# Attention's row of maxima: from sixteen products and four copies to one product, one copy and one transfer; three pairs loaded ahead

## The reference

```python
x = x + 0.5 * ffn(layernorm(x), w_router, w_gate, w_up, w_down)   # 32 experts, top 1, capacity 1.25
x = x + attn(layernorm(x), Wq, bq, Wk, bk, Wv, bv, Wo, bo)        # 16 heads of 32, rotary positions
x = x + 0.5 * ffn(layernorm(x), w_router, w_gate, w_up, w_down)
...
scores = einsum('bqhd,bkhd->bhqk', q, k) / sqrt(32)
attn = softmax(scores, axis=-1)
out = einsum('bhqk,bkhd->bqhd', attn, v)
```

## Time and profile before

| what | us |
|---|---|
| median of 3 runs (lowest, highest) | 4619.11 (4617.47, 4621.19) |
| the profiled execution's own time | 4617.62 |
| its span, first to last instruction | 4615.5 |
| TensorE busy in the span | 4359.8 (94%) |
| VectorE busy | 3248.9 (70%) |
| GpSimd busy | 2713.3 (59%) |
| ScalarE busy | 2237.3 (48%) |
| attention, from its first transfer to the first one of the next stage | 1572.4 to 3540.7 |

### The profile page before, as it was taken

One profiled execution on the slowest core, in us unless ns is written; L12 is line 12 of the kernel. 1 busy time (PEld: TensorE's weight loads), 2 busy tenths in 40 slices (PEclk: granted clock), 3 DMA queues, 4 the chain that ended last, 5 costly groups with the idle time before them and its releaser, 6 DMA issues. The chain is left out here.

```text
span 4615.5 us, 74660 instructions
## 1 busy us (share of the span) xinstructions
PE 4359.8 (94%) x26432; PEld 3108.5 (67%) x26432; DVE 3248.9 (70%) x6095; ACT 2237.3 (48%) x3667; POOL 2713.3 (59%) x1626
## 2 busy tenths in 40 slices
PE   7699999989999799999999999999996997999999
PEld 7689998968888554444444444444443886899998
DVE  7777777766766577777777777777772886777776
ACT  5543333322222167666666666666663443333333
POOL 2343444325555488888888888888885123444443
PEclk9999999989999799999999999999998997999999
DMA  5465555536555623443333344444333674555553
GB/s 184 137 213 183 183 183 181 182 130 185 172 178 178 158 46 89 93 93 91 88 90 85 88 92 93 93 91 92 82 88 134 220 247 151 184 183 185 186 185 122
DMA packets 471540, 650.34 MB, mean 141 GB/s; under 512 B 213277, under 2 KB 214577, under 8 KB 471201
## 3 DMA queue, kind: packets, MB, share of 16 engines
q1 hardware_dynamic: 440480, 579.32, 43.1%
q0 software_dynamic: 30720, 66.62, 3.8%
HBM read 468.75 MB, written 194.58 MB: 144 GB/s over the span
## 5 line engine op out<-in xcount | busy, mean ns | idle before, releaser
L1623 DVE TENSOR_REDUCE att_halves<-att_mx 128x1 f32<-128x512 f32 x2048 | 1276.4, 685 | 515.3 <-PE att_mx L1682 513.0
L1560 ACT ACTIVATE att_p<-att_st 128x512 f32<-128x512 f32 x2048 | 1119.2, 597 | 394.5 <-PE att_st L1702 382.1
L1512 POOL TENSOR_TENSOR att_pairsum<-att_p,att_p 128x1024 f32<-128x1024 f32 x512 | 1203.0, 2380 | 53.8 <-ACT att_p L1560 53.8
L1682 PE MATMUL att_mx<-att_k,att_q 96*128 96x512 f32 x2048 | 830.4, 410 | 67.2 <-DMA att_v<-v 66.2
L1702 PE MATMUL att_st<-att_q,att_k 128*128 128x512 f32 x2048 | 877.5, 430 | 14.2 <-ACT att_p L1560 8.8
L1702 PEld LDWEIGHTS att_st<-att_q,att_k 128*128 128x128 f32 x2048 | 387.4, 190 | 565.8 <-ACT att_p L1560 296.6
L1712 PE MATMUL att_op<-att_p,att_v 128*32 128x512 f32 x4096 | 545.7, 605 | 0.7 <-ACT att_p L1560 0.7
L1682 PEld LDWEIGHTS att_mx<-att_k,att_q 96*128 96x128 f32 x2048 | 395.3, 193 | 165.2 <-DMA att_v<-v 61.2
L800 DVE TENSOR_TENSOR e_w<-e_raw,e_w 128x2048 fp32r<-128x2048 f32 x192 | 439.1, 2287 | 41.9 <-ACT e_w L795 33.5
L819 ACT ACTIVATE e_sg<-e_gp 128x320 f32<-128x320 f32 x256 | 112.0, 438 | 731.6 <-PE e_up L182 669.0
L795 ACT ACTIVATE e_w<-e_raw 128x2048 fp32r<-128x2048 f32 x192 | 367.1, 1912 | 43.1 <-DMA e_raw<-in_w_gate 37.5
(11 more groups left out here) (154 smaller groups left out, 8544.0 us busy)
## 6 DMA issues: line engine op xcount, KB each, us to landing
e_raw<-in_w_gate SPq DMA_DIRECT2D x64, 1024.0 KB
e_raw<-in_w_up SPq DMA_DIRECT2D x64, 1024.0 KB
e_raw<-in_w_down SPq DMA_DIRECT2D x64, 1024.0 KB
att_q<-q SPq DMA_DIRECT2D x192, 256.0 KB, 4.2
att_k<-k SPq DMA_DIRECT2D x192, 256.0 KB, 6.2
r_ao<-ao SPq DMA_DIRECT2D x32, 1024.0 KB, 10.1
r_x<-in_x SPq DMA_DIRECT2D x16, 1024.0 KB, 8.0
x<-r_base SPq DMA_DIRECT2D x16, 1024.0 KB
```

What stands on the lines that cost most here:

```text
L1512: nc.gpsimd.tensor_tensor(out=pairsum[h][PLACE[g]][:, :], in0=pr[h][2 * g % RING][:, :], in1=pr[h][(2 * g + 1) % RING][:, :], op=ALU.add). ...
L1560: nc.scalar.activation(pr[h][kt % RING][:, half(c)], st[(4 * kt + x) % NB][:, :], ACT.Exp, scale=SCALE).then_inc(s_exp, 1)
L1623: nc.vector.tensor_reduce(out=halves[:, h, qt, c:c + 1], in_=mx[n % NB][:, :], axis=AX.X, op=ALU.max).then_inc(s_max, 1)
L1682: nc.tensor.matmul(mx[n % NB][:, :], qst[b][0:3 * HD, h, qt * P:(qt + 1) * P], kst[b][0:3 * HD, h, half(c)], start=True, stop=True).then_i ...
```

## The change

The maxima of a pair now lie in `big` as 16 columns without zeros between them. One product of these 128 x 16 with the identity gives 16 rows of 128 in `zp`. ScalarE copies them to a new tile `rowst` in SBUF (16 partitions x 128), waits for its own copy, and issues from its own queue one transfer that puts the 8 KB in order into partition 96 of `qst`. Partitions 97 to 127 of `qst` are set to zero once, before the first step. VectorE no longer copies. Score products wait for the transfer (`s_rowq`), totals for the copy (`s_rowc`).

SP's step is reordered: `give_sums` of pair p-1 first, then `load` of pair p+3 (before p+2), `take_inverse` of pair p-1 (before p-2), and `store` of pair p-2. VectorE's `invert` moves with it, from pair p-2 in turn 0 to pair p-1 after the fourth group of maxima of the second part of its step.

```diff
         pr = [[sb(f"p{h}_{t}", [P, L]) for t in range(RING)] for h in range(2)]
         pairsum = [[sb(f"pairsum{h}_{t}", [P, L]) for t in range(NZ)] for h in range(2)]
         halves = sb("halves", [P, 2, KT, 2])
-        big = S.pair(sb, "big", [P, 2, KT, HD])
+        big = S.pair(sb, "big", [P, 2, KT])
+        rowst = S.pair(sb, "rowst", [2 * KT, P], F32R)
         o = S.pair(sb, "o", [P, HALF])
         oh = S.pair(sb, "oh", [P, HALF], F32R)
         ol = S.pair(sb, "ol", [P, HALF], F32R)
...
         s_mx = sem("s_mx")
         s_max = sem("s_max")
         s_row = sem("s_row")
-        s_rowq = [sem(f"s_rowq{h}") for h in range(2)]
+        s_rowc = sem("s_rowc")
+        s_rowq = sem("s_rowq")
         s_st = sem("s_st")
         s_exp = sem("s_exp")
         s_add = sem("s_add")
...
 
             def step(i, b, left):
                 p = DEPTH * i + b
-                if left >= 2:
-                    load(*ahead(i, b, 2))
-                if p > 1:
-                    take_inverse(p - 2)
                 if p > 0:
                     give_sums(p - 1)
+                if left >= 3:
+                    load(*ahead(i, b, 3))
+                if p > 0:
+                    take_inverse(p - 1)
                 if p > 1:
                     store(p - 2)
 
-            load(0, 0)
-            load(0, 1)
+            for b in range(3):
+                load(0, b)
             rounds_out(DEPTH, NP, step)
-            take_inverse(NP - 2)
             give_sums(NP - 1)
             store(NP - 2)
             take_inverse(NP - 1)
...
         @block.gpsimd
         def _(pool):
 
-            for par in range(2):
-                nc.gpsimd.memset(big[par][:, :, :, :], 0.0).then_inc(s_memset, 1)
             nc.gpsimd.memset(ones[:, :], 1.0).then_inc(s_memset, 1)
-            pool.wait_ge(s_memset, 3)
             for b in range(DEPTH):
+                pool.wait_ge(s_memset, 1 + 2 * b)
                 nc.gpsimd.memset(kst[b][3 * HD:4 * HD, :, :].bitcast(F32), -1.0).then_inc(s_memset, 1)
+                pool.wait_ge(s_memset, 2 + 2 * b)
+                nc.gpsimd.memset(qst[b][3 * HD:4 * HD, :, :].bitcast(F32), 0.0).then_inc(s_memset, 1)
 
             def add(p, g, h):
 
...
                 nc.scalar.activation(pr[h][kt % RING][:, half(c)], st[(4 * kt + x) % NB][:, :], ACT.Exp,
                                      scale=SCALE).then_inc(s_exp, 1)
 
-            def copy_row(i, b, c):
-
-                act.wait_ge(s_row, DEPTH * i + b + 1)
-                nc.scalar.activation(qst[b][3 * HD:4 * HD, 1, half(c)], zp[tile(1, c), :],
-                                     ACT.Copy).then_inc(s_rowq[1], 1)
+            def copy_row(i, b):
+
+                p = DEPTH * i + b
+                act.wait_ge(s_row, p + 1)
+                act.wait_ge(s_rowq, past(16 * (p - 1)))
+                nc.scalar.activation(rowst[p % 2][:, :], zp[0:2 * KT, 0:P], ACT.Copy).then_inc(s_rowc, 1)
+                act.wait_ge(s_rowc, p + 1)
+                act.wait_ge(s_memset, 1 + 2 * DEPTH)
+                nc.scalar.dma_start(qst[b][3 * HD:3 * HD + 1, :, :].bitcast(F32),
+                                    rowst[p % 2][:, :].bitcast(F32)).then_inc(s_rowq, 16)
 
             def copy_o(p):
 
...
                             copy_z(p - 1)
                         if p > 1 and (kt, x) == (4, 3):
                             hi_o(p - 2)
-                        if left and kt in (ROW, ROW + 1) and x == 1:
-                            copy_row(*ahead(i, b, 1), kt - ROW)
-
-            for c in range(2):
-                copy_row(0, 0, c)
+                        if left and (kt, x) == (ROW, 1):
+                            copy_row(*ahead(i, b, 1))
+
+            copy_row(0, 0)
             rounds_out(DEPTH, NP, step)
             copy_o(NP - 1)
             copy_z(NP - 1)
...
         @block.vector
         def _(dve):
             dve.wait_ge(s_const, 16)
-            dve.wait_ge(s_memset, 3 + DEPTH)
+            dve.wait_ge(s_memset, 1 + 2 * DEPTH)
 
             def maxima(i, b, qt):
 
...
                 p = DEPTH * i + b
                 dve.wait_ge(s_max, NM * (p + 1) - 1)
                 dve.wait_ge(s_row, past(p - 1))
-                nc.vector.tensor_reduce(out=big[b % 2][:, :, :, 0], in_=halves[:, :, :, :], axis=AX.X,
+                nc.vector.tensor_reduce(out=big[b % 2][:, :, :], in_=halves[:, :, :, :], axis=AX.X,
                                         op=ALU.max).then_inc(s_max, 1)
-
-            def copy_row(i, b):
-
-                dve.wait_ge(s_row, DEPTH * i + b + 1)
-                for c in range(2):
-                    nc.vector.tensor_copy(qst[b][3 * HD:4 * HD, 0, half(c)], zp[tile(0, c), :]).then_inc(s_rowq[0], 1)
 
             def invert(p):
 
...
                 for qt in range(FIRST, KT):
                     if left:
                         maxima(*ahead(i, b, 1), qt)
-                    if qt == FIRST and p > 1:
-                        invert(p - 2)
                 if left:
                     join(*ahead(i, b, 1))
                 for qt in range(FIRST):
                     if left >= 2:
                         maxima(*ahead(i, b, 2), qt)
-                    if left and qt == ROW - TURN - 1:
-                        copy_row(*ahead(i, b, 1))
+                    if p > 0 and qt == FIRST - 2:
+                        invert(p - 1)
 
             for qt in range(KT):
                 maxima(0, 0, qt)
             join(0, 0)
-            copy_row(0, 0)
             for qt in range(FIRST):
                 maxima(0, 1, qt)
             rounds_out(DEPTH, NP, step)
-            for p in (NP - 2, NP - 1):
-                invert(p)
+            invert(NP - 1)
 
         @block.tensor
         def _(pe):
             pe.wait_ge(s_const, 16)
-            pe.wait_ge(s_memset, 3 + DEPTH)
+            pe.wait_ge(s_memset, 1 + 2 * DEPTH)
 
             def rough(i, b, n):
 
...
                 p = DEPTH * i + b
                 pe.wait_ge(s_max, NM * (p + 1))
                 pe.wait_ge(s_zo, past(p - 1))
-                for t in range(KT // 2):
-                    for h in range(2):
-                        for c in range(2):
-                            last = nc.tensor.matmul(zp[tile(h, c), t * P:(t + 1) * P], big[b % 2][:, h, c * (KT // 2) + t, :],
-                                                    ident[:, :], start=True, stop=True)
-                last.then_inc(s_row, 1)
+                nc.tensor.matmul(zp[0:2 * KT, 0:P], big[b % 2][:, :, :].rearrange("p h t -> p (h t)"), ident[:, :],
+                                 start=True, stop=True).then_inc(s_row, 1)
 
             def scores(p, b, kt, x):
                 h, c = x // 2, x % 2
                 if kt == 0:
-                    pe.wait_ge(s_rowq[h], 2 * p + c + 1)
+                    pe.wait_ge(s_rowq, 16 * (p + 1))
                 pe.wait_ge(s_exp, past(CH * p + prior(4 * kt + x) + 1))
                 nc.tensor.matmul(st[(4 * kt + x) % NB][:, :], kst[b][:, h, kt * P:(kt + 1) * P],
                                  qst[b][:, h, c * HALF:(c + 1) * HALF], start=True, stop=True).then_inc(s_st, 1)
...
                 pe.wait_ge(s_add, NA * p + READY[g])
                 if g == 0:
                     pe.wait_ge(s_zo, p)
-                    for h in range(2):
-                        pe.wait_ge(s_rowq[h], 2 * min(p + 2, NP))
+                    pe.wait_ge(s_rowc, min(p + 2, NP))
                 for h in range(2):
                     for c in range(2):
                         last = nc.tensor.matmul(zp[tile(h, c), :], ones[:, :], pairsum[h][g][:, half(c)],
```

## The result

| | us |
|---|---|
| before, median of 4 runs beside it | 4618.29 (4617.06 to 4621.19) |
| after, median of 4 runs | 4491.25 (4489.41 to 4492.87) |
| ratio | 0.9724, 95% interval 0.9707 to 0.9741 |
| predicted | 4494, range 4468 to 4542 |

The change is 127 us faster, and the forecast is 3 us off. The experiments show that the way to it was partly another one than the prediction told.

The account below looks back on a forecast made before the run. It took TensorE to bound the kernel. A step of 27.14 + 0.2 + 0.25 = 27.6 saves 2.0; 62 x 2.0 = 124 off 4617.6 gives 4493.6, with 1.5 to the median rounded to 4494 us; range 4468 to 4542.

Parts of the forecast that it names:

- TensorE bounds: Attention, kernel before: TensorE, busy 194 of 200 us, sets the time, with GpSimd close behind at 175.
- It bounded nothing itself: GpSimd's wait for the inverse, 3.8 us each, goes but set no time; ScalarE's `hi_o` stood 1.02 behind it.
- 27.14 for the turns: TensorE's eight turns of a step with nothing lost: five plain at 3.07 and three with totals at 3.93 us.
- the 0.94 goes entirely: Turn 3's wait for loads, 0.94 us a step, vanishes with loads three ahead, with 14 us to spare.
- The row: TensorE's sixteen products, 0.79 us, become one of 0.2 (bounds 0.1 and 0.45), saving 0.6 a step.
- Some 0.25 reach TensorE: Turn 5: of ScalarE's 1.5 us for copy, wait, issue and `hi_o`, 0.25 delays TensorE; bounds nothing and 0.9.
- In turns 6 and 7 nothing is left to lose: After turn 5, TensorE loses no more time to ScalarE in the step's last two turns.
- The 0.56 of the earlier trace: Kernel before, last three turns after the row: 9.77 us, 0.56 over plain, read as score products waiting for ScalarE.
- The transfer: The row's 8 KB lands 1.6 to 6.7 us after issue, within 7.0 allowed before the next pair's first score; costs nothing.
- GpSimd's floor: GpSimd's own work in a step, 26.0 us, stays under TensorE's new step, but only by 1.5.
- The ends: Beginning and end of attention: extra tile setting costs 4.6 us once, gains offset it; put at 0, within 5.
- The slower rival: Next pair's first score waits for a late row transfer; landing at 9.5 gives a 30.1 step, 4650 us; 4%.

Follow-up runs that it names:

- Kernels 1: The changed kernel's new row (one product, small copy, ScalarE's transfer) with SP's and VectorE's order of before; ratio 0.9997 to the kernel before.
- 3: The kernel before with only the loads issued three pairs ahead, at their old place; ratio 0.9981 to the kernel before.
- 9: The kernel before with loads three pairs ahead, issued behind the inverse of the same old pair; 4531.13 us, ratio 0.9807.
- 11: The kernel before with the scores' three PSUM buffers used in turn over the whole stage; ratio 0.9987 to the kernel before.
- kernel 8: The changed kernel with a second transfer of the same 8 KB issued from ScalarE, to a spare DRAM tensor; ratio 0.9799 to the kernel before.
- kernel 4: The changed kernel with ScalarE's small copy and its transfer's issue one turn later; ratio 0.9735 to the kernel before.
- Kernel 10: The kernel before with the inverse taken one pair earlier and VectorE's invert moved with it, loads still two ahead; 4737.64 us, ratio 1.0246.
- kernels 5: The changed kernel with each step's load issued ahead of the sums; ratio 0.9721 to the kernel before.

## Why the prediction was right, and where it was not

**Time and step: right.** 27.6 a step was forecast and 27.60 came over the same 62 intervals; 4494 against 4491.25.

**What bounds the kernel: wrong, the step that failed.** "TensorE bounds" rested on its busy share, and TensorE's waits were then summed as if each were its own. Of the inverse's wait the text says "It bounded nothing itself". Kernels 1, 3, 9 and 11 show that in the kernel before that wait was a link of the closed chain that set the step. That the sum came out right is in part luck, since the change happens to break the chain: after that TensorE does bound, and what is left of a step is what was counted from below, 27.14 for the turns, the row and a few tenths. The level reached was argued soundly, the split of the gain was not. By it the row alone would have been 37 us faster; measured was nothing. The two slips in its arithmetic are small: 4493.6 and 1.5 are 4495, not 4494, and 27.14 + 0.45 + 0.6 is 28.19, not 28.15, with 0.6 where ScalarE's bound had been 0.9.

**The loads and the inverse: half right.** Turn 3 fell to 3.93 and the waits for v and for the inverse went. But "the 0.94 goes entirely" holds only with the chain open; alone it gave 9.5 us.

**The row: right in size.** 0.17 in place, 0.21 for each further product, 0.2 forecast.

**ScalarE: right in sum, wrong in place.** The small copy took 0.27 (0.3 taken), the issue 0.51 (0.5 taken). By the formula of the Trainium skill ("ScalarE: Activation LUTs", What ACT_TABLE_LOAD costs) the copy is estimated at 0.29; this trace has 0.25 to 0.27, a little under. "Some 0.25 reach TensorE" in turn 5: nothing does, though kernel 8 shows that there is hardly any cover left. "In turns 6 and 7 nothing is left to lose": turn 7 loses 0.32, as it did before, from the buffers' restart. The 0.56 of the earlier trace rows that I gave to ScalarE's copies was 0.26 in turn 5 and 0.30 of this. The two errors cancel to 0.07, which is luck.

**The transfer: right.** 6.5 to landing against 6.7 as the upper row and 7.0 allowed; five short waits. Beside the loads it took 6.5 from its own queue, about what the inverse took behind them in theirs. The Trainium skill ("DMA: Bandwidth & Descriptors", Queues, rings and completion order) states that an engine alternates between queues packet by packet. If it did so here, these runs show no more gain from it than 6.5 for 6.7. Whether the transfer ran on two engines no run tells.

**GpSimd's floor: not reached.** It waits 99 us for exponentials over the middle of the stage, at 94% busy.

**The ends:** TensorE began at 1587.67 (1587.3 forecast), and the ends together gave 0.8, within the 5.

**The slower rival** did not come: it needed a landing of 9.0, and the longest of 64 was 7.4. Little was left before first scores would wait, 0.7 in the step shown, and kernel 4 prices that at 5 us. Kernel 10 shows a slower case that I had not thought of, by 117 us, from moving only one of the two things that SP's order moves.

## What to carry to other kernels

Before summing the waits of the busiest engine, follow one queue's rows once round: if each start is the end before it and the chain returns to itself in one period, that period is the step, and the busy engine's waits are only its remainder. Look also at the first steps of the loop: if they are shorter than the later ones, something else catches up. Break such a chain at the link that merely stands in line (here a small write behind big loads), then count what is left from below. And let buffers go round over the whole stage where the count of one pass is no multiple of them.

## What the runs showed of the hardware that was not expected

A transfer of 8 KB from ScalarE's queue landed in 1.8 us with no loads in flight and in 6.5 beside them (kernels 5 and the change), though its queue held nothing else; issued 3 us later it landed at nearly the same moment. Issuing it held ScalarE's queue for 0.51 us, longer than the 0.34 that SP needs for the 8 KB of sums, and the next exponential came 0.68 us after the copy.

TensorE's granted clock fell for single steps where TensorE waits: in no step of the change, in five of the kernel before (0.95), in 31 of 59 of kernel 10 (0.90 to 0.95). In the first of the five, TensorE had waited 2.03 us for v up to 2100.11, and the clock from 2100 to 2110 was 0.83.
